# A token embedding in two fp32r parts, beside an attention phase: patches and weights split for images 2 to 15, and a remainder written over its source

## The reference

```python
tokens = _patchify(x)                                  # 16 x 256 x 320
h = jnp.einsum('bnf,fd->bnd', tokens, W)               # 320 -> 256
h = (h - mean) * rsqrt(var + EPS) * gamma
h = h + attn(layernorm(h))    # 16 heads of 64, silu on q and k, decay from a running sum, no softmax
#   o normed per head over (tokens, 64), times gn_w, plus gn_b, times sigmoid gate, then Wo (1024 -> 256)
h = h + ffn(layernorm(h))     # 8 experts of hidden 1024, the best 2 of each token, weighted
```

## Time and profile before

| | us |
|---|---|
| median of 3 runs | 1326.96 |
| lowest and highest | 1323.49, 1327.07 |
| the profiled execution | 1323.79 |
| its span, first to last instruction | 1321.9 |
| TensorE busy in the span | 1250.9 (95%) |
| ScalarE, VectorE, GpSimd busy | 858.5, 825.2, 428.1 |
| mean granted clock | 0.983 |

### The profile page before, as it was taken

How to read it: one execution, slowest core, us unless ns; L and a number is a source line. 1 busy time by engine, 2 the same in 40 slices (tenths; PEclk the granted TensorE clock), 3 DMA queues, 4 the chain that set the end, 5 groups by cost and what they waited for, 6 DMA issues and landing times. The chain is left out here.

```text
span 1321.9 us, 27298 instructions
## 1 busy us (share of the span) xinstructions
PE 1250.9 (95%) x8534; PEld 1072.3 (81%) x8534; DVE 825.2 (62%) x2119; ACT 858.5 (65%) x2019; POOL 428.1 (32%) x524
## 2 busy tenths in 40 slices
PE   3899999999999999999999999999999999999996
PEld 2676777878778778778778778889999999989996
DVE  4455556665665665665665566657788888565552
ACT  2557577576576576576576565636788888666662
POOL 2021211241241241241141142164444544433434
PEclk7799999999999999999999999999999999999998
DMA  5321331341331331341332236458888787888873
GB/s 193 121 93 61 105 98 47 117 131 46 117 129 49 109 128 57 108 130 57 108 114 63 89 102 186 161 179 245 282 238 222 222 237 188 262 257 262 249 232 88
DMA packets 125607, 194.46 MB, mean 147 GB/s; under 512 B 16272, under 2 KB 91504, under 8 KB 125360
## 3 DMA queue, kind: packets, MB, share of 16 engines
q1 hardware_dynamic: 111920, 175.91, 41.5%
q0 software_dynamic: 13584, 17.26, 6.4%
HBM read 167.40 MB, written 29.05 MB: 149 GB/s over the span
## 5 line engine op out<-in xcount | busy, mean ns | idle before, releaser
L1161 PE MATMUL bank<-xn_sp,big_r 128*128 128x512 f32 x1152 | 312.1, 408 | 0.0
L1161 PEld LDWEIGHTS bank<-xn_sp,big_r 128*128 128x128 f32 x1152 | 204.6, 188 | 53.2 <-issue 1.4
L1674 DVE TENSOR_TENSOR att<-bank,dec_x 128x384 f32<-128x384 f32 x256 | 130.7, 552 | 110.1 <-PE bank L1198 108.9
L817 ACT ACTIVATE dec_x<-dec_x,ncum 128x256 f32<-128x256 f32 (+1 forms) x512 | 189.7, 444 | 5.7 <-POOL dec_x L654 5.7
L654 POOL TENSOR_SCALAR_AFFINE_SELECT dec_x<-dec_x 128x256 f32<-128x256 f32 x256 | 103.6, 434 | 215.8 <-DMA dec_x<-cum_scratch 215.7
L1494 PE MATMUL bank<-big_r 128*128 128x256 f32 x1296 | 168.0, 286 | 1.5 <-ACT mid_f L887 1.0
L1494 PEld LDWEIGHTS bank<-big_r 128*128 128x128 f32 x1296 | 160.5, 192 | 3.3 <-ACT mid_f L887 1.4
L705 POOL TENSOR_SCALAR mid_f<-mid_f,dec_x 128x256 f32<-128x256 f32 x71 | 76.9, 1087 | 187.0 <-DVE mid_f L1925 184.6
L711 POOL DMA_INDIRECT out<-mid_f,tok x71 | 118.6, 1671 | 53.0 <-POOL mid_f L705 22.0
L1941 DVE TENSOR_TENSOR big_r<-mid_f,big_r 128x256 fp32r<-128x256 f32 x216 | 91.4, 424 | 69.5 <-ACT big_r L907 69.3
L887 ACT ACTIVATE mid_f<-bank,h 128x256 f32<-128x256 f32 x216 | 101.2, 477 | 43.5 <-PE bank L1494 22.1
(11 more groups left out here) (217 smaller groups left out, 2231.4 us busy)
## 6 DMA issues: line engine op xcount, KB each, us to landing
big_f<-in_L_ffn_w SPq DMA_DIRECT2D x68, 1024.0 KB, 6.2
dec_x<-cum_scratch SPq DMA_DIRECT2D x128, 384.0 KB, 3.5
big_w<-in_L_ffn_w SPq DMA_DIRECT2D x12, 1024.0 KB, 6.7
mid_f<-expert_rows SPq DMA_DIRECT2D x27, 261.0 KB, 3.4
xt<-in_x SPq DMA_DIRECT2D x16, 256.0 KB, 3.7
h_scratch<-h SPq DMA_DIRECT2D x16, 256.0 KB, 2.3
h<-h_scratch SPq DMA_DIRECT2D x8, 512.0 KB, 4.3
out<-h SPq DMA_DIRECT2D x16, 256.0 KB, 4.0
```

What stands on the lines that cost most here:

```text
L817: act.activation(d, d, ACT.Exp, bias=ncum[p % 2][:, NS * u + s, 2 * c + hh:2 * c + hh + 1]).then_inc(M["exp_done"], 1)
L1161: mm = pe.matmul(bank[target][:, :], wp[:, k, c * P:(c + 1) * P], xp[:, k, :], start=(k == 0 and j == 0), stop=(k == EC - 1 and j == 2))
L1674: dve.tensor_tensor(att[hh][:, :], bank[4 + hh][:, 0:LW], dec[n % RING][:, hh, :], ALU.mult).then_inc(M["mult_done"], 1)
```

## The change

For images 2 to 15 (`WHOLE = 2`) patches and embedding weights are split into a high and a low fp32r part, and `tokens` makes three fp32r products in place of each fp32 one: 18 of 128x256 an image. Images 0 and 1 stay fp32.

- The high parts lie in the first 1,536 columns of `ys[0]`: `xt_hi` and `wt_hi`. The low parts are written over their sources: `xt_lo` is `xt`'s place as fp32r, `wt_lo` is `wt`'s.
- `patches_hi(n)` on ScalarE: two copies (128x512 and 64x256). `patches_lo(n)` on VectorE: two subtractions of the same sizes. For image 2p+3 they stand in c = 1, for image 2p+4 in c = 5, for image 2 in the start-up. The weights are split once there, with two casts of the zeroed rows.
- Since `ys[0]` is taken, y's high part goes to `ys[1]` and its low part over `osb` (`olo`). `keep_o` therefore waits for the projection that reads it (`wo_ps`), and so do the first loads over `osb`. w2's second set uses the two tensors in the other order.

```diff
-        y_sp = [y[:, :].rearrange("p (k n) -> p k n", k=GC) for y in ys]
+        y_hi_sp = ys[1][:, :].rearrange("p (k n) -> p k n", k=GC)
...
-        w2_sp = [parts((4096, 6144), 2048, HC), [y[:, :].rearrange("p (k n) -> p k n", k=HC) for y in ys]]
+        w2_sp = [parts((4096, 6144), 2048, HC), [y[:, :].rearrange("p (k n) -> p k n", k=HC) for y in (ys[1], ys[0])]]
...
+        xt_hi, wt_hi = (ys[0][:, i * (KT + 1) * S:(i + 1) * (KT + 1) * S].rearrange("p (k n) -> p k n", k=KT + 1) for i in range(2))
...
+        olo = big_lo[:, 4096:8192].rearrange("p (k n) -> p k n", k=NP)
...
                 if isinstance(k.b, int) and k.b < 2:
-                    sp.wait_ge(M["yl_done"], 4 * NPR - 2 + 2 * k.b)
+                    sp.wait_ge(M["wo_ps"], 4 * NPR - 2 + 2 * k.b)
...
+            def patches_hi(n):
+                act.wait_ge(M["xt_in"], 32 * (n + 1))
+                act.wait_ge(M["tok_ps"], n)
+                act.activation(xt_hi[:, 0:KT, :], xt[:, 0:KT, :], ACT.Copy).then_inc(M["xth_done"], 1)
+                act.activation(xt_hi[0:KREM, KT, :], xt[0:KREM, KT, :], ACT.Copy).then_inc(M["xth_done"], 1)
+
+            def token_weights_hi():
+                act.wait_ge(M["wt_in"], 32)
+                act.wait_ge(M["zeroed"], 2)
+                act.activation(wt_hi, wt[:, :, :], ACT.Copy).then_inc(M["wth_done"], 1)
...
-                have(act, "yl_done", 4 * (p - 1) + c // 2 + 1)
+                have(act, "wo_ps", 4 * (p - 1) + 2 * (c // GC) + 2)
...
-                act.activation(y_sp[0][:, 2 * j:2 * j + 2, :], osb[:, GC * g + 2 * j:GC * g + 2 * j + 2, :], ACT.Copy).then_inc(M["yh_done"], 1)
+                act.activation(y_hi_sp[:, 2 * j:2 * j + 2, :], osb[:, GC * g + 2 * j:GC * g + 2 * j + 2, :], ACT.Copy).then_inc(M["yh_done"], 1)
...
+                if c == 1 and main and nxt:
+                    patches_hi(2 * p + 3)
+                if c == 5 and main and pair(p + 2):
+                    patches_hi(2 * p + 4)
                 if c == 1 and nxt:
                     keep_xnT(2 * p + 2)
...
                     weight_hi(3)
+                    token_weights_hi()
+                    patches_hi(2)
...
+                else:
+                    pe.wait_ge(M["xtl_done"], 2 * (n - WHOLE + 1))
+                    pe.wait_ge(M["wtl_done"], 3)
+                    for s in range(NS):
+                        for k in range(KT + 1):
+                            for j, (wp, xp) in enumerate(three((wt_hi, wt_lo), (xt_hi, xt_lo))):
+                                mm = pe.matmul(bank[6][:, s * E:(s + 1) * E], xp[:, k, s * P:(s + 1) * P], wp[:, k, :],
+                                               start=(s == 0 and k == 0 and j == 0), stop=(k == KT and j == 2), skip_group_check=True)
...
-                        for q, (wp, yp) in enumerate(three(wo_sp, y_sp)):
+                        for q, (wp, yp) in enumerate(three(wo_sp, (y_hi_sp, olo[:, GC * g:GC * g + GC, :]))):
...
+            def patches_lo(n):
+                dve.wait_ge(M["xth_done"], 2 * (n - WHOLE + 1))
+                dve.tensor_tensor(xt_lo[:, 0:KT, :], xt[:, 0:KT, :], f32(xt_hi[:, 0:KT, :]), ALU.subtract).then_inc(M["xtl_done"], 1)
+                dve.tensor_tensor(xt_lo[0:KREM, KT, :], xt[0:KREM, KT, :], f32(xt_hi[0:KREM, KT, :]), ALU.subtract).then_inc(M["xtl_done"], 1)
+
+            def token_weights_lo():
+                dve.wait_ge(M["wth_done"], 1)
+                dve.wait_ge(M["tok_ps"], WHOLE)
+                for x in (xt_hi, xt_lo):
+                    dve.tensor_copy(x[KREM:P, KT, :], xt[KREM:P, KT, :]).then_inc(M["wtl_done"], 1)
+                dve.tensor_tensor(wt_lo[:, :, :], wt[:, :, :], f32(wt_hi), ALU.subtract).then_inc(M["wtl_done"], 1)
...
-                dve.tensor_tensor(y_sp[1][:, 2 * j:2 * j + 2, :], osb[:, cs, :], f32(y_sp[0][:, 2 * j:2 * j + 2, :]), ALU.subtract).then_inc(M["yl_done"], 1)
+                dve.tensor_tensor(olo[:, cs, :], osb[:, cs, :], f32(y_hi_sp[:, 2 * j:2 * j + 2, :]), ALU.subtract).then_inc(M["yl_done"], 1)
...
+                    if main and nxt:
+                        patches_lo(2 * p + 3)
...
                     if nxt:
                         log_decay(p + 1)
+                    if main and pair(p + 2):
+                        patches_lo(2 * p + 4)
...
             for c in range(NP):
+                if c == 6:
+                    token_weights_lo()
+                    patches_lo(2)
                 if c in (1, 3, 4, 6, 7):
                     weight_lo({1: 0, 3: 1, 4: 2, 6: 3, 7: 4}[c])
```

More of the change, by code:

```diff
@@ L134, in vit_layer @@
         xn_sp = [sb(f"xn_sp{j}", [P, EC, SP2], F32R) for j in range(2)]
+        with nc.sbuf_tensor("xt_lo", [P, KT + 1, S], F32R) as xt_lo:
+            pass
         xt = sb("xt", [P, KT + 1, S])
+        with nc.sbuf_tensor("wt_lo", [P, KT + 1, E], F32R) as wt_lo:
+            pass
         wt = sb("wt", [P, KT + 1, E])
+        xt_hi, wt_hi = (ys[0][:, i * (KT + 1) * S:(i + 1) * (KT + 1) * S].rearrange("p (k n) -> p k n", k=KT + 1) for i in range(2))
+        with nc.sbuf_tensor("big_lo", [P, 8192], F32R) as big_lo:
+            pass
         big_f = sb("big_f", [P, 8192])
+        olo = big_lo[:, 4096:8192].rearrange("p (k n) -> p k n", k=NP)
         stage_w = [big_f[:, i:i + 2048] for i in (0, 2048, 6144)]
@@ L275, in vit_layer @@
         passed mh_done zeroed c_in c_sum ws_in0 ws_in1 ws_in2 ws_hi ws_lo wt_in g_in
-        xt_in tok_ps s1_st s1_u s1_v0 s1_v1 s1_st2 s1_ve s1_rs s1_h s1_xn
+        xt_in xth_done xtl_done wth_done wtl_done tok_ps s1_st s1_u s1_v0 s1_v1 s1_st2 s1_ve s1_rs s1_h s1_xn
         s1_tps s1_xnT s1_aps s1_z h_out sp_abs sp_e sp_l sp_m sp_la gnh
@@ L337, in vit_layer @@
         EARLY = 5
+        WHOLE = 2
         SPAN = range(-2, NPR)
@@ L1110, in tokens @@
                     pe.wait_ge(M["s1_xnT"], n)
[L1111 to L1114, removed]
+                if n < WHOLE:
+                    for s in range(NS):
+                        for k in range(KT + 1):
+                            mm = pe.matmul(bank[6][:, s * E:(s + 1) * E], xt[:, k, s * P:(s + 1) * P], wt[:, k, :],
+                                           start=(s == 0 and k == 0), stop=(k == KT), skip_group_check=True)
+                else:
+                    pe.wait_ge(M["xtl_done"], 2 * (n - WHOLE + 1))
+                    pe.wait_ge(M["wtl_done"], 3)
+                    for s in range(NS):
+                        for k in range(KT + 1):
+                            for j, (wp, xp) in enumerate(three((wt_hi, wt_lo), (xt_hi, xt_lo))):
+                                mm = pe.matmul(bank[6][:, s * E:(s + 1) * E], xp[:, k, s * P:(s + 1) * P], wp[:, k, :],
+                                               start=(s == 0 and k == 0 and j == 0), stop=(k == KT and j == 2), skip_group_check=True)
                 mm.then_inc(M["tok_ps"], 1)
```

## The result

| | before | after |
|---|---|---|
| median, us | 1323.49 | 1326.46 |
| lowest to highest, us | 1321.26 to 1330.14 | 1324.20 to 1331.05 |
| profiled execution / its span, us | 1323.79 / 1321.9 | 1325.08 / 1322.0 |
| TensorE busy, us | 1250.9 | 1245.6 |
| VectorE busy, us | 825.2 | 843.2 |

Nineteen runs of each kernel on one chip give medians 3.0 us apart and a ratio of 1.0026 [1.0014, 1.0038], which is 3.4 us of 1323.49 with an interval of 1.9 to 5.0: slower, by less than 0.3%. TensorE is busy for 5.3 us less and the kernel is longer all the same.

A forecast was written before the change was run, and what follows sets the result against it. TensorE, 98% busy, was taken as the bound, with VectorE's chain at c = 5 holding it up. Tokens -3.2, c = 7 0, c = 5 +4.8 and start-up +2.0 gave +3.6 us: 1329.5 named, own range 1326 to 1333, with rivals 1322.5 to 1337.

The forecast's parts named there:

- Tokens, -0.45 us an odd image: TensorE at c = 2, images 3 to 15: 18 fp32r products take 2.23 us instead of 2.68, 3.2 us saved in all.
- The rule of the Trainium skill: Tokens: true fp32 takes four passes, so 24 become 18, an estimated 0.67 us an image; rival built on it, chance 0.10.
- Even images, 0: Images 4 to 14 at c = 7: shorter tokens only lengthen the wait for ScalarE's keep_o copy; 0 of 2.7 us gained.
- c = 1, 0: Splits for images 3 to 15: hidden in VectorE's idle time for TensorE, with 0.6 us left; cost 0.
- c = 5, +0.8 us a pair: VectorE's subtractions delay gsc and the decayed products, and TensorE follows one for one; six pairs, 4.8 us.
- The rival of 1.5 us: At c = 5 the split meets GpSimd's masking and costs 1.5 us, six times; total 1335 us, chance 0.22.
- my 0.15 for them: At c = 5: 0.15 us added to gsc's 0.65 us delay, within a price range of 0.5 to 1.5 us.
- ScalarE's slip: Before tanh_q at c = 5: ScalarE's own queue slips some 0.35 us and recovers in c = 6.
- Start-up, +2.0 us: Five VectorE instructions before ncum delay it 2.3 us; queries 1.7 us later, plus 0.3; between 1.0 and 3.5 us.
- the 0.3 that I had added: Start-up: 0.3 us added because TensorE's clock, which rose near 47, may now rise later.
- y's part, 0: y_lo over its source, keep_o and late loads waiting for wo_ps, w2's tensors swapped: cost 0.
- The level: Base time: sum 1327.4 us on the profiled execution, 1330.6 on the median of three runs; 1329.5 named between them.

The follow-up runs named there:

- e2: Kernel after, with VectorE's subtractions and ScalarE's copies for images 4 to 14 moved from c = 5 into c = 6; median 1324.00 us, 0.9989 of before.
- e5: Kernel before, with ScalarE's keep_o(p, 6) put first at c = 7; median 1318.69 us, 0.9964 of before.
- e6: Kernel after, with ScalarE's keep_o(p, 6) put first at c = 7; median 1320.88 us, 0.9968 of before.
- e1: Kernel after, with only VectorE's subtractions for images 4 to 14 moved behind gated(p, 0, 0) at c = 6; median 1325.74 us, 1.0009 of before.
- e4: Kernel before with only y's part of the change and the wo_ps waits, embedding all in fp32; median 1323.10 us, 0.9996 of before.
- e3: Kernel after, with image 2 back in fp32 and the weights split at c = 1 of pair 0; median 1327.72 us, 1.0029 of before.
- e8: Kernel after, repeated unchanged as yardstick; median 1327.47 us, 1.0016 of before.

## Why the prediction was right

Its central claim, that three terms come to a small loss, held: +3.6 us was named for the change, and the runs show +3.0 between the medians, +3.4 [1.9, 5.0] by the ratio. The traces show each term; the runs alone couldn't tell them apart.

- **Tokens, -0.45 us an odd image.** Measured 2.68 - 2.24 = 0.44, and e2, with its costs moved away, gives 0.42 a period. The rule of the Trainium skill that would have made it 0.67 (FP8 and Floating Point Precision, TensorE Precision Notes: true fp32 takes four passes) isn't borne out as a time: 18 products took 0.84 of what the fp32 ones took, not 0.75. The output projection's pitch was the right guide.
- **Even images, 0.** The wait went from 0.42 to 0.86 us: all of the gain. e5 and e6 show the cause: with `keep_o` taken first the 0.44 comes back.
- **c = 1, 0.** Subtractions start at 272.20 and end at 273.31, and VectorE still idles 0.54 us before the decayed products (0.6 was named).
- **c = 5, +0.8 us a pair.** Measured 0.84. Its parts were shared out otherwise than I had it: the first subtraction started where I put it, 1.41 us behind the scores; the two took 1.16 us instead of 1.0, since the 64x256 one took 0.62 where 0.43 was assumed; and the small ones took the 1.00 us that they took before, so my 0.15 for them was wrong. The two errors cancel, and that is luck. The rival of 1.5 us named the right place, since it is this subtraction that stretches beside GpSimd, but only one of the two does and by 0.2.
- **The step that was missing.** I counted ScalarE's slip as harmless (0.35 us at tanh_q, made up in c = 6). It delays `keep_x2` from 1.41 us behind the pair's scores to 2.24, and TensorE waits for that. The wait lies under VectorE's longer one and adds nothing in the kernel after, so the sum came out right without it; e1 uncovered it. Had I proposed e1's cure from the prediction alone, I would have promised 0.84 us and got 0.32.
- **Start-up, +2.0 us.** VectorE's delay 2.34 (2.3 named), tokens(2) 3.98 (4.15), queries 1.6 us later against logits (1.7), and first weighted products 2.24 us later, 1.9 by the means of all profiles. Tokens(2) begins 2.4 us later in every profile with this start-up. The clock rose at 50.8 us instead of 47.2, as feared, and over six profiles of each start-up it rises 16.0 us behind logits(0) instead of 14.6; but in e1, with the changed start-up, it rose at 14.7, so the 0.3 that I had added is neither shown nor refuted.
- **y's part, 0.** e4 shows it, within its interval of 0.9981 to 1.0012.
- **The level.** The one number that was off by its size is the base. The profiled sum was 1327.4, and I moved it up to 1329.5 for a median of three runs, 1326.96. Nineteen runs of the kernel before give 1323.49, with the profiled execution's 1323.79 in the middle of them; 1323.49 + 3.6 = 1327.1, beside 1326.46 measured, which is 3.0 us under the 1329.5 named and near the low end of the range. A median of three, on a kernel whose runs spread over 9 us, was weaker evidence than I took it for.

Period: 100.7 named, 100.76 found. The terms by the rows: 2.24 (start-up) + 6 x (0.84 - 0.44) - 0.44 (image 15) = 4.2 us at the end of the attention phase, 3.9 with the start-up's mean, inside the runs' interval for the whole. Behind it one profile shows nothing of this size, as waits for DMA that differ from profile to profile are as large (last section).

## What to carry to other kernels

On an engine that is 98% busy a cheaper instruction pays only where that engine doesn't stop for another one right behind it: look for the bracket after the shortened stretch, and if another engine's copy ends last there, move that copy first. The work that an edit puts on helper engines costs the more: 1.2 us of subtractions that seemed to fit into an idle time of 1.6 us cost 0.84, because they could start only after two copies, which ended 0.3 us before that gap was over. And behind the wait that ends last look for the second one, a few tenths below it, before promising what a cure gives back. A stage read from one middle pair leaves out the last ones: the longest wait for `keep_o`, 3.21 us, stands in pair 6.

## What the hardware showed beyond that

**A two-input operation beside GpSimd.** The 64x256 subtraction (VectorE's line, all 14: ns minimum/median/maximum), in the kernel after:

```profile
L1658 DVE TENSOR_TENSOR xt_lo<-xt,y_sp x14: 407/616/624, 41.4 to 675.9; 64x256 fp32r<-64x256 f32 x14
```

It takes 0.61 to 0.62 us in the eight places where one of GpSimd's maskings (L663) runs beside it, which are all six at c = 5 and two at c = 1, and 0.41 in the six others. GpSimd loses too: the four maskings of pair 2 at c = 5 take 1.98 us instead of 1.49, and it is the two beside the subtractions that are longer, 0.72 and 0.58 us instead of 0.41. The Trainium skill (GPSIMD Engine Reference, Specifications) says that GpSimd's SBUF interfaces are shared with VectorE, with contention for operations of two SBUF inputs; these rows agree, and give it a size for this subtraction: half as long again. The 128x512 one just before it kept its usual 0.69 us, though the first masking starts 0.45 us before its end; there it was the masking that took longer. At c = 1 this one took 0.77 to 0.92 us in five of seven places. Before the change this had its price too: gsc, gd and gbi take 0.35, 0.33 and 0.32 us here beside the maskings, and 0.17 each at 359 to 360 us, where no masking runs (gd and gbi stand beside another operation of GpSimd there, L660).

**TensorE's clock in mid-kernel.** Behind 700 us the granted clock falls to 0.50, for 3.4 us as a rule, at places that change from one profile to the next. In the kernel before:

```profile
730.00:740.00 10.00, 7.17 (x37) 5.07 (x38) 7.53 (x11) 5.24 (x9) 2.30 (x5) 0.83 0.66 215
764.00:774.00 10.00, 8.05 (x43) 6.25 (x42) 6.40 (x22) 5.19 (x13) 0.77 (x2) 0.83 0.18 60
```

In the kernel after:

```profile
733.00:743.00 10.00, 6.79 (x40) 4.82 (x36) 6.51 (x10) 5.70 (x9) 0.77 (x2) 0.83 0.54 170
764.00:774.00 10.00, 8.08 (x57) 6.05 (x55) 5.84 (x24) 7.39 (x23) 3.16 (x5) 1.00 0.32 98
```

A clock of 0.83 over 10 us is one such stretch at the 1.2 GHz level. The kernel before has two, after one, e3 three (at 736, 773 and 1169 us, the first 6.8 us long). In the twelve profiles each fall between 700 and 1300 us lies inside an idle time of TensorE of 1.8 to 3.2 us or up to 1.2 us behind its end. The first of them, at 732 to 737 us, is in every one of the seven profiles with the old order at c = 7, where TensorE idles 3.21 us for `keep_o` in pair 6, and in none of the five with `keep_o(p, 6)` first, where it idles 1.31. A second idle time, for VectorE's `att`, is 1.8 to 2.0 us long in every profile (it ends at 767.7 us in the kernel before), and the clock falls there in seven of the twelve. What decides at such a place whether it falls stays open.

**Two profiles with the same span.** From the start of the span the kernel after is 4.3 us behind at pair 7's first scores (750 us), and 3.0 behind at 833, the last weighted product (attention reaches past the 760 us named above): the second stretch of before lies between. The remaining 3 us close between 1140 and 1310 us, where TensorE waits for the DMA that brings the tokens' rows to an expert. Its waits there, before and after:

```profile
PE bank L1276 <- DMA mid_f<-expert_rows: 7.6, 5, 2.6
```
```profile
PE bank L1311 <- DMA mid_f<-expert_rows: 4.0, 5, 1.2
```

This isn't the change's doing as far as the other profiles tell: e8, the kernel after once more, has 5.4 us of these waits and a span of 1324.6, and e4, whose attention phase is as long as before's, has 4.6. So one profile of each kernel can't tell 1 or 2 us of change by its span. Why the DMA comes later in one profile than in another stays open.
